# Decoder layer on one core: a gate moved by one chunk in the scan, and the memory stage in another order

## Time and profile before

| what | value |
|---|---|
| three runs | 621.09, 623.63, 626.03 us; median 623.63 |
| the profiled execution | 625.76 us, of it the profile's span 624.0 us |
| busy, of the span | PE 577.9 us (93%), DVE 401.4 (64%), ACT 328.4 (53%), POOL 172.4 (28%) |
| the scan | about 99 to 200 us of the span |
| the memory stage | about 200 to 249 us; its retrieval until about 284 us |

### The profile page before, as it was taken

One profiled execution on the slowest core, in us unless ns is written; L12 is line 12 of the kernel. 1 busy time (PEld: TensorE's weight loads), 2 busy tenths in 40 slices (PEclk: granted clock), 3 DMA queues, 4 the chain that ended last, 5 costly groups with the idle time before them and its releaser, 6 DMA issues.

```text
span 624.0 us, 14105 instructions
## 1 busy us (share of the span) xinstructions
PE 577.9 (93%) x4830; PEld 457.4 (73%) x4831; DVE 401.4 (64%) x997; ACT 328.4 (53%) x711; POOL 172.4 (28%) x190
## 2 busy tenths in 40 slices
PE   7999999898998898987999999998999999999995
PEld 5444457776777565554788888887888999999994
DVE  4986697999999692465456655658766454444441
ACT  3887995877876612356665665564422223332220
POOL 1300006677675401741000000000412332222221
PEclk9999989999999999898999999999999999999998
DMA  7100034564650862007100000043601111111100
GB/s 254 54 1 0 17 102 147 161 194 144 194 163 17 296 258 71 1 1 230 42 18 19 19 11 19 19 154 79 187 17 36 35 33 34 36 33 34 29 17 0
DMA packets 47293, 49.53 MB, mean 79 GB/s; under 512 B 7622, under 2 KB 41642, under 8 KB 47242
## 3 DMA queue, kind: packets, MB, share of 16 engines
q1 hardware_dynamic: 41882, 43.65, 21.9%
q0 software_dynamic: 2208, 5.14, 2.9%
q10 hardware_dynamic: 3152, 0.07, 0.3%
HBM read 39.24 MB, written 5.26 MB: 71 GB/s over the span
## 4 chain that ended last, share of the span: by engine, by line
PE 65%; DVE 18%; issue 7%; ACT 7%; DVEq 1%; POOL 1%; ACTq 0%; POOLq 0%
PE banks L2351 12%; PE banks L2340 12%; PE banks L1808 7%; DVE arena L1257 4%; PE banks L2191 4%; DVE arena L1233 3%; PE banks L2092 3%; PE banks L2216 3%; PE banks L2223 2%; PE banks L2236 2%; PE banks L2103 2%; PE banks L2232 2%; PE banks L1842 2%; DVE ybuf L1474 2%; DVE arena L1243 1%
## 5 line engine op out<-in xcount | busy, mean ns | idle before, releaser
L1053 ACT ACTIVATE prob_b<-banks,gate_w 128x128 f32<-128x128 f32 x92 | 26.3, 368 | 112.0 <-PE banks L2340 111.7
L2351 PE MATMUL banks<-arena,prob_b 128*128 x368 | 83.2, 379 | 0.9 <-issue 0.9
L2340 PE MATMUL banks<-ybuf 128*128 128x128 f32 x560 | 79.3, 276 | 1.9 <-DVE ybuf L1695 1.9
L2351 PEld LDWEIGHTS banks<-arena,prob_b 128*128 128x128 f32 x368 | 68.2, 190 | 9.5 <-issue 1.1
L2340 PEld LDWEIGHTS banks<-ybuf 128*128 128x128 f32 x560 | 71.8, 192 | 3.4 <-DVE ybuf L1695 2.5
L1808 PE MATMUL banks<-featT,ybuf 128*128 128x512 f32 x160 | 70.2, 594 | 1.1 <-ACT featT L692 1.1
L1474 DVE TENSOR_REDUCE ybuf<-banks 128x12 f32<-128x1848 f32 (+1 forms) x32 | 46.1, 1441 | 16.5 <-PE banks L2191 16.5
L1808 PEld LDWEIGHTS banks<-featT,ybuf 128*128 128x128 f32 x160 | 29.8, 190 | 36.6 <-issue 35.0
L1182 DVE SCALAR_TENSOR_TENSOR arena<-arena,conv_w 128x512 f32<-128x512 f32 x72 | 48.9, 743 | 11.3 <-ACT arena L706 11.3
L653 POOL DMA_INDIRECT out<-featT,dts x23 | 23.1, 1005 | 116.2 <-DVE featT L1735 115.9
L624 POOL TENSOR_TENSOR xres<-xres,ybuf 128x256 f32 (+1 forms) x16 | 12.6, 787 | 130.4 <-DVE ybuf L1494 130.4
(11 more groups left out here) (404 smaller groups left out, 1247.3 us busy)
## 6 DMA issues: line engine op xcount, KB each, us to landing
arena<-cum_rows SPq DMA_DIRECT2D x16, 512.0 KB, 4.6
arena<-W1T SPq DMA_DIRECT2D x8, 1024.0 KB, 11.9
arena<-W2T SPq DMA_DIRECT2D x8, 1024.0 KB, 8.8
arena<-arena SPq DMA_DIRECT2D x16, 320.0 KB, 3.2
featT<-ecum_rows SPq DMA_DIRECT2D x30, 128.0 KB, 3.0
xres<-x SPq DMA_DIRECT2D x4, 512.0 KB, 11.1
x_rows<-xres SPq DMA_DIRECT2D x16, 128.0 KB, 2.2
ybuf<-attn_in_wT SPq DMA_DIRECT2D x1, 1288.0 KB, 7.2
```

Source lines behind the costliest of these rows:

```text
L1053: i = act.activation(hidT[:, p, f, :], bank[2 * p + 1][:, (f - 4) * P:(f - 3) * P], ACT.Relu, bias=b1_cols[:, ds(e * NFF + f, 1)])
L2340: m = pe.matmul(bank[2 * p + half][:, f * P:(f + 1) * P], w1_now[k][p][:, (4 * half + f) * P:(4 * half + f + 1) * P], xsT[:, p, k, :], sta ...
L2351: m = pe.matmul(bank[4 + p][:, 0:D], hidT[:, p, f, :], w2_of[:, ds(e * NFF + f, 1), :].rearrange("p a n -> p (a n)"), start=(f == 0), stop ...
```

## The change

Three things are altered. In the scan, `gate(t)` is cut in two: the skip (`add_skip(t)`) stays where it was, and the product with `silu(z)` moves behind the scalings of the next chunk but one step later, `gate(t - 1)` in step t; the mask of `gmat` moves behind it, into `mask_sides`, and raises `sides_ready` in place of the second scaling. In the scores, tanh's table is loaded earlier by a one-column instruction, and `score_rows(0)`, `turn_scores(0)` and the copies of turned y change places. In the memory stage, `select(b)` produces the selected rows turned, in 16 products of 50 columns in place of 8 of 256, so that `keep_rows` and `turn_pool` go; `values_of(1)` moves behind `select(1)` and `keep_values(0)` behind the second ranking; `memory_sides` is cut in `memory_keys` and `memory_values`, with `head(1)` between them for sequence 1; and DVE keeps half of the values of sequence 1.

```diff
             def make_m(t, p):
                 pool.wait_ge(S("decay_mat"), t + 1)
-                pool.wait_ge(S("g_ready"), t + 1)
+                pool.wait_ge(S("sides_ready"), t + 1)
...
             scale_y((9, 11, 13))
+            act.activation(red[:, 0, 0:1], eps_col[:, :], ACT.Tanh)
             keep_hidden(0)
             scale_y((15,))
             keep_yT(4)
+            tanh_scores(0)
             keep_yT(6)
-            tanh_scores(0)
...
-            def keep_rows(b):
+            def keep_pool(b):
                 act.wait_ge(S("select_mm"), b + 1)
-                act.activation(pool_rows[0:POOL, b, :], bank[4 + b][0:POOL, P:P + D], ACT.Copy).then_inc(act_once, reached(f"pool_rows_{b + 1}"))
-
-            def keep_pool(b):
-                act.wait_ge(pe_once, at(f"pool_turned_{b + 1}"))
...
-                for j in range(2):
+                for j in range(2 - b):
...
-            keep_rows(0)
             keep_pool(0)
             keep_sides(0)
-            keep_rows(1)
...
-                if wait:
-                    dve.wait_ge(S("m_ready"), t - 1)
-                dve.tensor_tensor(gmat[:, p, :], bank[1][:, P:2 * P], tri_le[:, :], ALU.mult).then_inc(S("g_ready"), 1)
...
-                i.then_inc(S("sides_ready"), 1)
+
+            def mask_sides(t, p, wait):
+                if wait:
+                    dve.wait_ge(S("m_ready"), t - 1)
+                dve.tensor_tensor(gmat[:, p, :], bank[1][:, P:2 * P], tri_le[:, :], ALU.mult).then_inc(S("sides_ready"), 1)
...
             def dve_step(t, p, wait=True):
                 chunk_sides(t + 1, 1 - p, True)
+                gate(t - 1, 1 - p, wait)
+                mask_sides(t + 1, 1 - p, True)
                 sum_y(t, p)
                 add_state(t)
-                gate(t, p, wait)
+                add_skip(t, p)
...
-            keep_yT(7)
...
             half_plus(0)
+            keep_yT(7)
...
             place_tokens(0)
-            keep_values(0)
             score_cols(1)
             for k in range(TB):
                 rank_tile(1, k)
             place_tokens(1)
+            keep_values(0)
             keep_values(1)
             dve.wait_ge(S("mean_ready"), B)
+
+            def keep_gate_values():
+                dve.wait_ge(S("val_mm"), B)
+                for r in (slice(0, POOL), slice(HP, HP + POOL)):
+                    i = dve.tensor_scalar(vals[r, 1, D:2 * D], VAL_BANK(1, 1)[r, D:2 * D], mean_s[r, 1, 1:2], None, ALU.mult)
+                i.then_inc(S("vals_ready"), 1)
...
             turn_y(5)
+            pe.wait_ge(dve_once, at("w2b_ready"))
+            score_rows(0)
             turn_y(6)
             turn_y(7)
-            pe.wait_ge(dve_once, at("w2b_ready"))
-            score_rows(0)
+            turn_scores(0)
             score_hidden(1)
-            turn_scores(0)
...
-                for k in range(TB):
-                    m = pe.matmul(bank[4 + b][0:POOL, P:P + D], onehot[:, b * TB + k, :], y_tok[:, b * TB + k, :],
-                                  start=(k == 0), stop=(k == TB - 1))
+                for c in range(KD):
+                    for k in range(TB):
+                        m = pe.matmul(bank[4 + b][:, 3 * P + 64 * c:3 * P + 64 * c + POOL], y_tok[:, b * TB + k, c * P:(c + 1) * P], onehot[:, b * TB + k, :],
+                                      start=(k == 0), stop=(k == TB - 1))
...
-            values_of(1)
...
             head(0)
             select(1)
+            values_of(1)
+            memory_keys(1)
             pe.wait_ge(S("vals_ready"), 1)
             head(1)
-            turn_pool(1)
             pe.wait_ge(S("v_main_ready"), B)
             pe.wait_ge(S("v_tail_ready"), B)
-            memory_sides(1)
-            pe.wait_ge(S("vals_ready"), B)
+            memory_values(1)
+            pe.wait_ge(S("vals_ready"), B + 1)
```

More of the change, by code:

```diff
@@ L1252, in add_state, with add_skip @@
                 dve.tensor_tensor(state, state, bank[6][:, :], ALU.add).then_inc(S("state_added"), 1)
-            def gate(t, p, wait):
+            def add_skip(t, p):
                 dve.wait_ge(S("intra_added"), t + 1)
@@ L1259, in gate @@
                 i.then_inc(S("y_ready"), 1)
+            def gate(t, p, wait):
                 if wait:
@@ L1283, in _ @@
                 dve_step(2 * i + 2, 0)
+            gate(NT - 2, 0, True)
             sum_y(NT - 1, 1)
+            add_skip(NT - 1, 1)
             gate(NT - 1, 1, True)
@@ L2015, in select, with memory_keys @@
                 pe.wait_ge(S("onehot_ready"), b + 1)
-                for k in range(TB):
-                    m = pe.matmul(bank[4 + b][0:POOL, P:P + D], onehot[:, b * TB + k, :], y_tok[:, b * TB + k, :],
-                                  start=(k == 0), stop=(k == TB - 1))
+                for c in range(KD):
+                    for k in range(TB):
+                        m = pe.matmul(bank[4 + b][:, 3 * P + 64 * c:3 * P + 64 * c + POOL], y_tok[:, b * TB + k, c * P:(c + 1) * P], onehot[:, b * TB + k, :],
+                                      start=(k == 0), stop=(k == TB - 1))
                 m.then_inc(S("select_mm"), 1)
-            def turn_pool(b):
-                pe.wait_ge(act_once, at(f"pool_rows_{b + 1}"))
-                for c in range(KD):
-                    m = pe.transpose(bank[4 + b][:, 3 * P + 64 * c:3 * P + 64 * c + POOL], pool_rows[0:POOL, b, c * P:(c + 1) * P], ident[0:POOL, 0:POOL])
-                m.then_inc(pe_once, reached(f"pool_turned_{b + 1}"))
-            def memory_sides(b):
+            def memory_keys(b):
                 pe.wait_ge(act_once, at("w_val_kept"))
@@ L2037, in memory_sides @@
                         for i in range(2):
-                            m = pe.matmul(bank[VAL_BANK[b]][HP * i:HP * i + POOL, j * D:(j + 1) * D], pool_tokT[:, b, k, :], w[:, k, :],
+                            m = pe.matmul(VAL_BANK(b, j)[HP * i:HP * i + POOL, j * D:(j + 1) * D], pool_tokT[:, b, k, :], w[:, k, :],
                                           start=(k == 0), stop=(k == KD - 1))
```

27 lines of the change are left out of this document (16 added, 11 removed).

## The result

The changed kernel takes **638.92 us** (median of 4 runs, 635.83 to 644.24), beside 623.83 us for the kernel before in the same session (621.09 to 626.03): ratio 1.025, 95% interval [1.017, 1.033]. I had said 624.8, with a range from 618 to 631. The profiled execution took 635.83 us with a span of 634.1, 10.1 us over the span of before, while the medians lie 15.1 us apart. The 5 us between the two come from which executions were profiled: that of the changed kernel is the fastest of its four, 3.1 us under their median, and that of before lies 1.9 us over its own.

What follows compares the result with a forecast made beforehand. DVE's queue was taken to bound the scan, with a chain of engines from there to the retrieval. Scan -0.7 and memory stage +1.8 on the profiled 625.76 gave 626.9, a median of 624.8 us, range 618 to 631.

Steps and rivals of the forecast that it cites:

- What bounds: Scan: DVE's queue bounds at 6.45 us a chunk, 0.9 of it held by POOL; PE's floor is 5.77.
- The holds of the three other instructions: Scan: POOL's L506, L520 and L522 hold DVE's skips, 1.18 us a chunk, giving 6.4 us.
- L515 then stands at 2.6 to 3.65 us after L1252 and lets go some 0.7 us ahead of the gate: Scan: POOL's state decay ends before the gate starts, so the largest old hold, 0.58 us, goes.
- The rival for this side: Scan: the decay lies over the gate, up to 0.9 us a chunk, +8.4 us, 633 in all; chance 0.09.
- The memory stage to `turn_attn(0)`: Selection, new wait, keys, head and values on PE: `turn_attn(0)` forecast at 250.95 for 249.19.
- The wait: Memory stage: after `values_of(1)` PE idles 2.6 us for ACT's copy of sequence 1's pooled tokens.
- The sum, +1.8: Memory stage: forecast delay of `turn_attn(0)`, 1.8 us, shifting everything behind it.
- my lower bound: Selection: 3.57 us for its 16 products, from 16 products of 128 columns in the experts; 4.0 was forecast.
- POOL's padding and adds start 2.7 us later, and have 2 us of idle in each pair to catch up.: Retrieval, behind `turn_attn(0)`: POOL's 2.7 us delay was expected to be caught up in idle time.
- The clock, "moved, 0": PE's loss at 1.2 GHz behind idle, 1.6 us, was taken to move to the new idle: net 0.
- Two sums: Scan: first skip's hold put at 0.43 us; 5.25 us of DVE work plus 1.18 put at 6.4, -0.7 us.
- The chance: Whole kernel: probability given to a result slower by over 1%, 0.09.

Runs made afterwards that it cites:

- decay_behind_skips: The changed kernel with POOL's state decay made to wait for the last skip of the chunk before: 630.25 us, ratio 1.008.
- memory_only: The kernel before with only the change's part on scores, selection and values, the scan as before: 630.67 us, ratio 1.012.
- scan_only: The kernel before with only the scan's part of the change, gate behind the next chunk's scalings and mask behind the gate: 636.54 us, ratio 1.019.
- gate_only: The kernel before with the gate alone moved behind the next chunk's scalings, the mask left ahead of them: 639.76 us, ratio 1.024.
- memory_both: The kernel before with the change's memory part, ACT's copy of pooled tokens ahead of the exponentials and POOL's four adds ahead of the padding: 621.20 us, ratio 0.994.
- change_mended: The changed kernel with the decay behind the skips, and ACT's copy and POOL's adds moved ahead: 624.97 us, ratio 0.999.

## Why the prediction was wrong

- **What bounds.** Right: DVE's queue bounds the scan, in this order as in the old one, and only instructions with two operands in SBUF stretch. Every chunk of the table is DVE's own time plus such holds.
- **The holds of the three other instructions.** Right: 1.18 us and 6.4 us a chunk, without the decay, against 1.15 and 6.38 in `decay_behind_skips`.
- **"L515 then stands at 2.6 to 3.65 us after L1252 and lets go some 0.7 us ahead of the gate".** This is the step that failed. The place was right: L1249 starts at 143.84 and L516 at 146.41, which is 2.57. But I asked only whether the decay reaches the gate. By my own terms the four skips, 1.06 + 1.18 us with their holds, ran from 0.6 to 2.84 after L1252, the last of them from about 2.55. The decay at 2.6 falls on it. It began 0.03 us after the skip and held it for 0.88 us (1.22 for 0.34). The eleven chunks from the fifth on take 7.27 us for 6.45, +8.9. That is nearly the +9.1 at the scan's end; what else moved there (the second copy 1.6 us earlier, 1.0 us more in the next three chunks, 0.8 more behind the last copy) adds up to 0.2. The rival for this side had the right price and the wrong victim: up to 0.9 us a chunk, to be paid by the gate. The gate itself is clear of it: the decay ends at 147.45, and the gate starts at 148.92.

  The trace of the kernel before had the case, here in its chunk of 7.19 us: a fourth skip, and POOL's decay, which starts 0.006 us after it.

```profile
143.30 1.20 DVE L1257 SCALAR_TENSOR_TENSOR arena<-arena,d_cols 128x128 f32<-128x128 f32 x1
```

```profile
143.30 1.04 POOL L515 TENSOR_TENSOR arena<-arena,dts 128x512 f32<-128x512 f32 x1 [0.34 <-PE banks L1904]
```

  I read the holds from the chunks at 129.31 and 135.08, and let the mean stand for the rest. The two longest, 8.03 and 7.19 us, both have a fourth skip held by the decay (1.13 and 1.20 us): the price and the victim stood there.
- **The sum of squares as cover.** I placed the decay by PE's product alone, and left out that POOL itself has to be free. L521 and L523 keep it busy until 146.31, and the state's product (L1917, from 145.16) is through 0.1 us before. The decay starts at once: POOL's four instructions now run in one row behind the mask. That fits the collision repeating to 0.01 us, where the decay waited 0.34 to 0.92 us for PE before; it was not tried by itself. That both ways of placing the decay gave the same 2.6 us is luck.
- **The memory stage to `turn_attn(0)`.** The wait was right to 0.03 us. The sum, +1.8, measured -0.1, and -0.4 in `memory_only`. `select` cost 3.51 us from start to start, 247.53 less 244.02, where I took 4.0 from the keys' side: 16 products at 0.22 us, just under my lower bound. That is 0.5 us, twice. Another 0.7 was gained on the way: `select(1)` starts 34.8 us after the last projection, where my 236.1 less 200.15 is 35.95. The Trainium skill's figure ("TensorE: Matmul & The Clock Gate", "LDWEIGHTS"), worked out to an estimate of 3.4 us, was nearer than the row that I chose.
- **"POOL's padding and adds start 2.7 us later, and have 2 us of idle in each pair to catch up."** Wrong for the first pair, and the second step that failed. The rows of the kernel before that I should have read, POOL and DVE:

```profile
250.32 4.94 POOL L602 TENSOR_TENSOR xres<-xres,ybuf 128x512 f32<-128x512 f32 x4
256.04 1.27 POOL L614 TENSOR_TENSOR xres<-xres,prob_b 128x512 f32<-128x512 f32 x1 [0.77 <-DVE prob_b L1431]
```

```profile
255.27 0.69 DVE L1431 SCALAR_TENSOR_TENSOR prob_b<-prob_b,banks 128x512 f32<-128x512 f32 x1 [3.57 <-ACT prob_b L926]
```

  There POOL was through with its adds 6.1 us after `turn_attn(0)`, and the update 6.8: 0.8 us of slack, and that only because `head(2)` ran in some 3.5 us at a granted clock of 0.63. Now the update was ready 5.1 us after `turn_attn(0)`, and POOL 7.0. DVE waited 2.68 us, PE 1.82. A slow stretch had hidden this wait. `scan_only` shows it with the old memory stage: there `head(2)` ran at a clock of 1.00, and DVE waited 1.76 us for POOL:

```profile
266.57 0.75 DVE L1446 BATCH_NORM_STATS2 stats<-xres 128x6 f32<-128x256 f32 x2 [1.76 <-POOL xres L614]
```

  So 0.9 us of the 2.68 are the change's own. A slow stretch came back behind the wait, at 268.
- **The clock, "moved, 0".** Right in the profiled execution, by luck: the stretch behind `turn_attn(0)` is gone, none stands behind the new wait, and one of the same price (3.68 us for 2.29) came at 268, behind a wait that I had not seen.
- **Two sums.** The first skip's hold is 0.2 + 2.18 - 1.99 = 0.39 us, not 0.43, and 5.25 + 1.18 is 6.43, 0.3 us off the scan and not 0.7. Neither changes the reading.
- **The chance.** 0.09 for slower by over 1%. An exclusion of 0.9 us, fourteen times over, with a margin of 0.7 us, deserved far more.

The Trainium skill ("SBUF — State Buffer", "Who interferes with whom") says that issue order decides who of the two blocks. The trace agrees where the starts are apart (`gate_only`: L506 0.6 us ahead, and the gate held for 1.6 us). Within 0.03 us it differs, as far as the recorded starts give the order: DVE's skip has the earlier start and is the one that is held.

## What to carry to other kernels

When two engines exclude each other for whole instructions, write both queues of a period on one time axis, with the holds in, and look at every meeting, not at the one that the change is about. An instruction that starts together with a victim can cost nearly its full length in every period (0.88 of 1.04 us here); one more wait that makes it late, into work that it doesn't disturb, took 0.88 us out of 7.27. And a copy that waits for nobody belongs ahead of one that waits for another engine: exchanging two lines was worth 2.6 us. And read the longest period of a loop as well as the mean: the collision to come stood in it.

## What the hardware showed that I had not expected

- The tie. A skip that starts 0.027 us ahead of POOL's decay is held for 0.88 us; one that starts 0.044 us ahead (in `scan_only`) is not held, and the decay takes 1.20 us for 1.04. In the kernel before a skip that starts 0.006 us ahead is held (at 143.30), and a gate that starts 0.004 us ahead is not (at 130.89).
- The hold follows the other instruction's length, 0.43 us less for a decay that is 0.43 us shorter, and is 0.16 us shorter than that instruction both times.
- Products of 50 columns with a weight of 128 x 128 cost 0.22 us each in a row of 16; the keys' side, four in 1.00 to the next start, gave 0.25.
- The same memory stage kept a granted clock of 1.00 from 208 to 304 us in `memory_both`, and had three 8 us stretches between 0.58 and 0.71 in `change_mended`: `turn_attn(0)` at 243.88 in the one and 251.76 in the other, with the same end of the scan.
